# Adaptive-norm feed-forward with routed low-rank experts on one core: the order of a sweep step's five matrix products

## The reference

```python
base   = x @ W.T                                            # x: 2048 tokens x 1024
logits = x @ Wr.T + 5 * one_hot(language)                   # 8 experts
gates  = softmax over the top 2 of logits, else 0
y      = base + 2 * sum_e gates[:, e] * (x @ A[e].T) @ B[e].T   # rank 16 each, 128 in all
dots   = softmax(y @ centroids.T / 0.1)                     # 64 clusters
hits   = dots > 0.01
row    = any(hits, over clusters);  col = any(hits, over tokens)[assignments]
out    = x + where(row & col, y @ V.T + bias, 0)            # V: 1024 x 1024
```

## Times and profile before

| | us |
|---|---|
| median of 3 runs | 334.92 (334.3 to 335.08) |
| the profiled execution | 334.6 |
| its span | 332.6 |
| TensorE busy | 328.7 (99%) |
| VectorE busy | 262.5 (79%) |
| ScalarE busy | 137.4 (41%) |
| data moved | 48.05 MB, mean 144 GB/s |

### The profile page before, as it was taken

How to read it: one execution, slowest core, us unless ns; L and a number is a source line. 1 busy time by engine, 2 the same in 40 slices (tenths; PEclk the granted TensorE clock), 3 DMA queues, 4 the chain that set the end, 5 groups by cost and what they waited for, 6 DMA issues and landing times.

```text
span 332.6 us, 4597 instructions
## 1 busy us (share of the span) xinstructions
PE 328.7 (99%) x1756; PEld 288.0 (87%) x1756; DVE 262.5 (79%) x477; ACT 137.4 (41%) x232; POOL 1.0 (0%) x9
## 2 busy tenths in 40 slices
PE   8999999999999999999999999999999999999996
PEld 6888889999999999999877888888888888888886
DVE  4838967258988988989996979679398594997995
ACT  5824655245765664755633313232223331331310
POOL 1000000000000000000000000000000000000000
PEclk9999999999999999999999999999999999999999
DMA  7956600433523333335511372805508237060113
GB/s 266 415 177 236 237 3 0 135 121 126 191 101 142 138 128 126 128 124 217 230 67 61 125 253 84 281 15 201 180 1 290 90 130 248 0 242 12 63 66 126
DMA packets 14070, 48.05 MB, mean 144 GB/s; under 512 B 1696, under 2 KB 1952, under 8 KB 14048
## 3 DMA queue, kind: packets, MB, share of 16 engines
q1 hardware_dynamic: 14048, 47.75, 39.7%
HBM read 39.36 MB, written 8.39 MB: 144 GB/s over the span
## 4 chain that ended last, share of the span: by engine, by line
PE 98%; DMA 1%; DVE 0%; SPq 0%; issue 0%
PE ps L1054 26%; PE ps L1056 26%; PE ps L1055 26%; PE ps L1128 8%; PE ps L1064 7%; PE ps L1130 4%; DMA wq_raw<-in_wq 1%; PE ps L1141 1%; PE ps L1148 0%; PE ps L1150 0%; PE ps L1203 0%; DVE nat L1047 0%; SPq L330 0%; DVE wq_hi L660 0%; PE ps L1198 0%
## 5 line engine op out<-in xcount | busy, mean ns | idle before, releaser
L1054 PE MATMUL ps<-vt_hi,w_hi 128*128 128x288 f32 (+1 forms) x184 | 58.7, 319 | 0.0
L1055 PE MATMUL ps<-vt_lo,w_hi 128*128 128x288 f32 (+1 forms) x184 | 58.0, 315 | 0.0
L1056 PE MATMUL ps<-vt_hi,w_lo 128*128 128x288 f32 (+1 forms) x184 | 58.0, 315 | 0.0
L425 ACT ACTIVATE u<-ps 128x512 f32<-128x512 f32 x31 | 18.5, 597 | 81.2 <-PE ps L1056 54.6
L1055 PE MATMUL ps<-gop_lo,sl_s_hi 128*128 128x512 f32 x128 | 49.8, 389 | 0.0
L1128 PE MATMUL ps<-aw,xt_hi 128*128 128x400 f32 x128 | 38.9, 365 | 0.0
L1054 PE MATMUL ps<-gop_hi_t,sl_s_hi 128*128 128x512 f32 x96 | 37.4, 390 | 0.0
L1056 PE MATMUL ps<-gop_hi_t,sl_s_lo 128*128 128x512 f32 x96 | 37.3, 389 | 0.0
L1055 PEld LDWEIGHTS ps<-vt_lo,w_hi 128*128 128x128 f32 x184 | 34.6, 188 | 1.6
L1054 PEld LDWEIGHTS ps<-vt_hi,w_hi 128*128 128x128 f32 x184 | 34.5, 188 | 1.6
L1056 PEld LDWEIGHTS ps<-vt_hi,w_lo 128*128 128x128 f32 x184 | 34.5, 188 | 1.5
(11 more groups left out here) (143 smaller groups left out, 657.8 us busy)
## 6 DMA issues: line engine op xcount, KB each, us to landing
xt_raw<-in_xt SPq DMA_DIRECT2D x32, 512.0 KB, 4.0
nat<-in_x SPq DMA_DIRECT2D x16, 512.0 KB, 4.2
out<-nat SPq DMA_DIRECT2D x15, 512.0 KB, 2.7
w_raw<-in_w SPq DMA_DIRECT2D x7, 512.0 KB, 3.2
wraw<-in_w SPq DMA_DIRECT2D x5, 512.0 KB, 4.3
vt_raw<-in_v SPq DMA_DIRECT2D x4, 576.0 KB, 5.4
vt_raw<-in_v SPq DMA_DIRECT2D x4, 256.0 KB, 3.9
wq_raw<-in_wq SPq DMA_DIRECT2D x4, 256.0 KB, 4.3
```

The costliest lines, as they stand in the source:

```text
L425: return nc.scalar.activation(dst, src, ACT.Copy)
L1054: nc.tensor.matmul(dst, l_hi, r_hi, start=start, stop=False, skip_group_check=True)
L1055: nc.tensor.matmul(dst, l_hi, r_lo, start=False, stop=False, skip_group_check=True)
L1056: return nc.tensor.matmul(dst, l_lo, r_hi, start=False, stop=stop, skip_group_check=True)
```

## The change

On TensorE both halves of G's block come first in a step, then the turn, token product 0, the logits product and token product 1. On ScalarE the high part of x tile 0 is made at the head of the step that uses it, ahead of `router_exp`, no longer at the end of the step before; `r_part` or `t_part` follows `router_exp`; `evict(n, 1)` comes ahead of `keep_hgt`. On VectorE both low parts of x come right behind `route`, then `t_sums` in even steps, then the rests of the turned gates and of w, and `softmax_max`; `r_rest` or `t_rest` stands between `softmax_max` and `softmax_hits`. SyncE's queue, the arithmetic and the waits of each piece are as they were.

```diff
--- before.py
+++ after.py
@@ -531,23 +531,20 @@
             for n in range(NPAIR):
                 if n >= 1:
                     take_rest(n - 1)
+                    split_x(0, n)
+                    router_exp(n - 1)
                     if n >= 2 and n % 2 == 0:
                         r_part(row_of(n - 1) // 2, slice(A1, HALF), chunk_number(n - 1, 1))
                     elif n >= 2:
                         t_part(n // 2 - 1, row_of(n - 2) // 2)
-                    router_exp(n - 1)
                 evict(n, 0)
                 if n >= 1:
                     split_x(1, n)
+                evict(n, 1)
+                if n >= 1:
                     keep_hgt(n - 1)
                     split_w_again(n + 1)
-                evict(n, 1)
-                if n >= 1:
                     keep_logits(n - 1)
-
-                if n + 1 < NPAIR:
-                    split_x(0, n + 1)
-                if n >= 1:
                     softmax_exp(n - 1)
 
             def keep(dst, bank, i, free, kept):
@@ -806,22 +803,20 @@
                 nc.vector.tensor_reduce(qsel[:, 2 * n:2 * n + 2], hits[:], AX_X, ALU.max).then_inc(soft, 1)
                 nc.vector.tensor_tensor(hit_sum[:], hit_sum[:], hits[:], ALU.add).then_inc(soft, 1)
 
-            split_x(0, 1)
             for n in range(1, NPAIR):
                 route(n - 1)
+                split_x(0, n)
+                split_x(1, n)
                 if n >= 2 and n % 2 == 0:
                     t_sums(KH + n // 2 - 1, row_of(n - 1) // 2, slice(A1, HALF), chunk_number(n - 1, 1))
+                split_hgt(n - 1)
+                split_w_again(n + 1)
+                softmax_max(n - 1)
+
+                if n >= 2 and n % 2 == 0:
+                    r_rest(KH + n // 2 - 1, row_of(n - 1) // 2, slice(A1, HALF))
                 elif n >= 2:
                     t_rest(n // 2 - 1, row_of(n - 2) // 2, slice(0, 4))
-                split_hgt(n - 1)
-                split_x(1, n)
-                split_w_again(n + 1)
-                if n >= 2 and n % 2 == 0:
-                    r_rest(KH + n // 2 - 1, row_of(n - 1) // 2, slice(A1, HALF))
-                softmax_max(n - 1)
-
-                if n + 1 < NPAIR:
-                    split_x(0, n + 1)
                 softmax_hits(n - 1)
 
             def s_sums(i):
@@ -1153,10 +1148,10 @@
 
             for n in range(NPAIR):
                 chunk(n, 0)
-                token_product(0, n)
+                chunk(n, 1)
                 if n >= 1:
                     turn_hg(n - 1)
-                chunk(n, 1)
+                token_product(0, n)
                 if n >= 1:
                     lora_logits(n - 1)
                 token_product(1, n)
```

## The result

The changed kernel takes 336.52 us (median of 6 runs, 336.06 to 336.73), the kernel before 335.0 beside it. The ratio is 1.0054, with an interval of 1.0043 to 1.0065: slower by 1.4 to 2.2 us. The forecast was 337.0, slower, in a range of 335.4 to 338.2.

What follows compares the result with a forecast made beforehand. TensorE was taken as the bound, busy 11.70 of 11.70 us a step. Stalls 1.72 + S slab 0.44 + order 0 = 2.16 us over the 334.92 median gave 337.1, stated as 337.0, range 335.4 to 338.2.

Steps and rivals of the forecast that it cites:

- TensorE's own order: TensorE's five pieces permuted within a sweep step: cost 0, bounds -0.08 and +0.08 us a step, +-0.6 over seven steps.
- The loads and ScalarE's queue: Sweep: x0 and w loads go out together, ScalarE's x0 copy moves to the step's head; both hidden, some 0.4 us in hand.
- The pause and the T rest: VectorE, odd steps: T rest of 2.28 us in a pause of at most 1.13; next routing starts at T + 2.15.
- The stalls: Logits product waits for the turned gates' rest behind the T sums: 0.86 us each in steps 4 and 6, none in step 2.
- The third stage's S slab: First S product of the third stage: VectorE leaves the sweep 1.33 us later, so the product starts 0.44 us later.
- the prediction's estimate: VectorE operations each costing their whole record: 0.4 to 0.5 us more per stall, 338.0 us; not adopted in the forecast.
- Worse: Rival: x0 or x1 lands late, step 2 stalls 0.3 too, the last x slab is late; 337.9 us, chance 0.17.
- Half: Rival: S slab or half of each stall missing, as operations close up in a full queue; about 336.0 us, chance 0.11.
- Not slower: Rival: VectorE's delay never reaches TensorE at the turned gates' rest in steps 4 and 6; 334.4 to 335.4 us, chance 0.17.

Runs made afterwards that it cites:

- the last kernel: Changed kernel with the T rest in two halves and VectorE's x tile 1 low part moved behind the T sums or first half: 334.47 us, ratio 1.0004.

## Why the prediction was right

**TensorE's own order, forecast 0 with bounds of 0.6.** Confirmed: +0.02 a step, 0.15 in all, where nothing waits (the last kernel). Token product 0 behind the turn takes 2.40 to 2.42, as taken from the row of token product 1.

**The loads and ScalarE's queue, hidden.** Confirmed: x0 landed in 3.3 us with the w load behind it. In no step did TensorE wait for x0 in the changed kernel.

**The pause and the T rest.** Confirmed by place, and by taking it out, halving it and lengthening it. The routing start of the even steps was forecast at 2.15 and was 2.07: the forecast put the T rest at its record, 2.28, and the distance to the next start is 2.21. It also allowed the pause at most 1.13, and the T rest found 0.97 in it; since the forecast laid the T rest end to end behind the maximum, that bound doesn't enter the sum.

**The stalls, forecast 0.86 each in steps 4 and 6 and none in step 2.** The places were right; the size was 0.68. Three terms were too large by small amounts. The T sums took 1.73 to the next start (107.94 to 109.67) where I had 1.84, from 1.80 and an added 0.04. An operation that doesn't need the sums, the turned gates' rest, starts 0.08 before their record ends. The R rest, which in the kernel's code waits for them, starts 0.03 after it (150.92 to 152.76), and that distance is the 1.84. The routing start was 0.08 earlier. And the handover from VectorE to TensorE was 0.05 (110.09 to 110.14) where I took 0.14 from the kernel's first matmul. Against them, the logits product takes 0.47 after a stall (110.14 to 110.61) and 0.38 to 0.39 without one (97.83 to 98.22 in step 3), 0.09 more. Sum 0.86 - 0.11 - 0.08 - 0.09 + 0.09 = 0.67.

**The third stage's S slab, forecast 0.44.** It was 0.34, with VectorE 1.26 late and not 1.33, and a handover of 0.11 (164.27 to 164.38).

**The sum.** 2.16 forecast, as 1.72 + 0.44 + 0 for the order; 1.82 measured in the trace, as 1.36 + 0.34 + 0.12. So the mechanism and its places were right. The stalls and the slab were taken too large, 2.16 for 1.70, and the 0.12 of the order, well within its bounds of 0.6, brought the sum nearer by chance. The forecast erred by adding records where distances between starts were wanted, and by taking one handover, the kernel's first, for all of them. In the medians the change cost 1.5 us against 335.0 and 2.2 against 334.36, so they alone could not have told 1.8 from 2.2.

The Trainium skill says that the next operation waits until the pipe has emptied (VectorE: DVE Perf Modes, section "The DRAIN you can't avoid"). The same section adds that an operation that isn't held starts earlier, which the prediction left out. Taken as the end of the record, the first sentence would have given more still, 338.0 by the prediction's estimate; the row at 107.94, 1.81 us long with the next start 1.73 later, speaks against that reading here and agrees with the addition.

**The rivals.** "Worse" had a late x1 stall step 2. Late landings came, but in steps 4 and 7. In the changed kernel step 4 was late anyway, and in step 7 VectorE waited 0.58 us for x1's high part and then still 0.71 for the turned gates. Its mechanism is real: it is the 0.13 and 0.51 of the kernel with the T rest moved ahead, and the 0.23 of the one with halves. "Half" named the right kind of error, operations that close up in a full queue, but it took off 0.34 us in all and not half of each stall. "Not slower" is out: 0.85 us less between logits and hits was never there.

## What to carry to other kernels

Where one engine is already full, a new order has next to nothing to win and can add waits. List the new due times of its pieces first. Then walk the queue of the second busiest engine against them through two steps, since a delay made in one kind of step can be paid in the next kind. A pause takes an operation of its own length and no longer one; the excess is carried over, so cut the operation or put something without a due time behind it, and put what others wait for ahead of sums that nobody wants yet. Sum a queue by the distances between starts, not by records, and take a distance from a place where the next operation needs as much of the one ahead as in yours.

## What the runs showed of the hardware

**Late landings.** The x load issued at the beginning of steps 4 and 7 landed 4.2 to 4.4 us after issue in the changed kernel, both times that it was profiled, and in the experiments that moved the T rest, its halves, the sums or x1's low part; their other x loads took 3.0 to 3.8. In the kernel before two x loads took 4.1 and 4.4, one of them in step 7. Over all ten traces 16 x loads of the sweep took 4.1 us or more, and behind the issue of each of them, by 0.3 to 1.3 us, a packet of the instruction queue started (at 102.06 in the changed kernel, for a load issued at 100.82). Of the x loads without a packet of that queue so near, none took over 3.8. But four loads with one landed in 3.4 to 3.8 us. So the late landings go with these packets; that the packets cause them no run here shows.

**A wait costs a little more than its length.** After a wait of 0.6 us the four small logits products took 0.09 us longer than without one, nearly all of it at the first, at a full granted clock. It is as much after a short wait: 0.47 us for the four in step 4 of the kernel with halves, where they start 0.15 late, and in step 4 of the kernel with the T rest ahead, where they start 0.04 late.

**From VectorE to TensorE.** From the end of VectorE's last operation to the start of the product that waits for it, it was 0.05 us for the logits product and 0.11 for the first S product; the kernel's first product had 0.14.
